# Attention edge layer: a third row and index buffer, and a block's steps taken in another order

## The chip, the cores and the metric

The kernel is one program on one core of a Trainium2 chip. The metric is device time in microseconds (us); lower is better. Engines are named as the profile names them: PE is TensorE (PEld its weight loads), DVE is VectorE, ACT is ScalarE, POOL is GpSimd, SP is SyncE.

## What is computed

Four graph layers run over the same 106,250 edges, sorted by destination, and 6,250 nodes. The change touches the edge part of the second, a graph attention layer with 8 heads:

```python
h = (x @ W.T).reshape(n, heads, out_dim)
a_s = jnp.sum(h * att_src, axis=-1)
a_d = jnp.sum(h * att_dst, axis=-1)
logits = jax.nn.leaky_relu(a_s[src] + a_d[dst], NEG_SLOPE)
m = jax.ops.segment_max(logits, dst, num_segments=n)
e = jnp.exp(logits - m[dst])
den = jax.ops.segment_sum(e, dst, num_segments=n)
alpha = e / (den[dst] + 1e-16)
out = jax.ops.segment_sum(alpha[:, :, None] * h[src], dst, num_segments=n)
```

## The kernel before, in words

`edges_gat` (L1017) takes the edges in 832 tiles of 128; 4 tiles are a group, 4 groups are a block, so there are 52 blocks. A node's edges stand together. All 16 tiles of a block are worked on together in its maxima; all else goes group by group.

For each block, POOL issues 16 indirect gathers (L1118), one a tile: 128 rows of 264 floats, the 256 features and the 8 source logits. Group b may be gathered into a buffer once `windows` has used the group b that lay there (L1112 to L1113). Then:

- **One-hots.** DVE's `select` (L1219) makes a 128x128 one-hot for each tile, edge against destination within the tile's window of 128 nodes. PE's `transpose` (L1393) turns it, ACT's `copy_sel` (L1133) copies the turned group out of PSUM, and PE's `expand` (L1401) multiplies it with the window's rows (loaded by SP, L1093) into destination logits in `att_ps`.
- **Maxima.** ACT copies the source logits (`copy_src`, L1162), PE's `values` (L1355) turns them, DVE's `tile_maxima` (L1231) scans them, PE's `tile_ends` (L1359) and DVE's `carries` (L1241) pass maxima from tile to tile, PE's `carry_lanes` (L1365) and DVE's `maxima` (L1254) finish them, PE's `edge_maxima` (L1371) turns them back. DVE's `logits_of` (L1271) forms logit minus maximum; ACT's `weights` (L1146) is the exp. PE's `falls` and `spread` and ACT's `shrink` make the factor by which a node that began in the block before is rescaled.
- **Sums.** DVE's `message` (L1289) multiplies a group's rows by the weights. PE's `windows` (L1413) multiplies rows and weights by the one-hots into `psa`, one PSUM bank a tile, 4 tiles. DVE's `add` (L1298) adds each of the four banks to the window in the accumulator `acc`; for group 0 it rescales one column first. `psa` has no second buffer: `windows` of a tile waits for the `add` of the same tile four tiles before.

Every engine runs its own hand-written order, tied to the others by semaphores. In a step, c is the coming block (one-hots), m the block in its maxima, a the one before m. `staggered` (L166) runs the steps in a hardware loop of two steps a turn, after two that stand outside it. The order on DVE before is: select c0; message a3; add a1; tile_maxima m; add a2; carries m; select c1; add a3; maxima m; select c2; logits_of m; select c3; message m0, m1, m2; add m0. PE follows it, with windows a2 and a3 at the head of its step and windows m0 and m1 at its end.

Of the kernel before, what the change touches and what calls it, by code (L numbers as in the profile page):

```python
# [28 lines left out]
PLANES = KH + 1  # L29
TILES = 832  # L30
# [135 lines left out]
def staggered(eng, step, lag, count=CHUNKS, peel=PEEL):  # L166


    def outside(s):
        step(lambda j: Chunk(s - j) if 0 <= s - j < count else None)  # L170

    for s in range(peel):
        outside(s)
    with eng.Fori(0, (count - peel) // 2) as pairs:
        for q in range(2):
            step(lambda j: Chunk(peel + q - j, pairs))
    for s in range(count, count + lag):
        outside(s)
# [838 lines left out]
def edges_gat(nc, dram, sh, acc):  # L1017
# [4 lines left out]
    with Phase(nc, "l1") as ph:  # L1022
# [3 lines left out]
        one = ph.sb("one", [HEADS, TILES])  # L1026
        pass_on, pass_back = ph.sb("pass_on", [HEADS, 2, TILES]), ph.sb("pass_back", [HEADS, TILES])
        rows = [ph.sb(f"rows{i}", [P, SEG, DW]) for i in range(2)]
        idx = [ph.sb(f"idx{i}", [P, SEG], I32) for i in range(2)]
        sel = [ph.sb(f"sel{i}", [P, SEG, P]) for i in range(2)]  # L1030
        wx = [ph.sb(f"wx{i}", [P, SEG, P]) for i in range(2)]
# [25 lines left out]
        gathered = [S(f"gathered{i}") for i in range(2 * NB)]  # L1057
# [7 lines left out]
        val_done = S("val_done", 1)  # L1065
# [9 lines left out]
        win_done = S("win_done", 2 * NB * GT)  # L1075
        added = S("added", GT)

        ph.begin()
        with nc.Block() as block:
# [24 lines left out]
            @block.gpsimd  # L1104
            def _(pool):
                def indices(n, q):
                    nc.gpsimd.tensor_copy(idx[q][:, :], sh["src_sb"][:, bass.ds(n * SEG, SEG)]).then_inc(idx_done, 1)

                def tiles(n, q, more):
                    hold(pool, ph, idx_done, n + 1)  # L1110
                    for b in range(NB):
                        hold(pool, ph, win_done, (n * NB + b + 1) * GT)  # L1112
                        if b == NB - 1 and more:  # L1113
                            hold(pool, ph, val_done, n + 1)
                            indices(n + 1, 1 - q)
                        for t in range(GT):
                            j = b * GT + t
                            nc.gpsimd.indirect_dma_start(  # L1118
                                out=rows[q][:, j, :], out_offset=None, in_=dram["tab1"][:, :],
                                in_offset=bass.IndirectOffsetOnAxis(ap=idx[q][:, j:j + 1].bitcast(U32), axis=0),  # L1120
                            ).then_inc(gathered[q * NB + b], 16)

                indices(0, 0)
                with pool.Fori(0, ITERS // 2 - 1) as pair:
                    for q in range(2):
                        tiles(pair * 2 + q, q, True)
                for q in range(2):
                    tiles(ITERS - 2 + q, q, q == 0)

            @block.scalar  # L1130
            def _(act):
# [14 lines left out]
                def weights(c):  # L1146
                    act.wait_ge(logits, c.n + 3)
                    nc.scalar.activation(wx[c.p][:, :, 0:HEADS], diff[c.p][:, :].rearrange("p (t h) -> p t h", h=HEADS),
                                         ACT.Exp).then_inc(w_done, 1)
# [12 lines left out]
                def copy_src(c):  # L1162
                    for b in range(NB):
                        act.wait_ge(gathered[c.p * NB + b], c.k * 64 + 64)
                    act.wait_ge(logits, c.n + 1)
                    nc.scalar.activation(src_v[c.p][:, :].rearrange("p (t h) -> p t h", h=HEADS), rows[c.p][:, :, D:DW],
                                         ACT.Copy).then_inc(src_done, 1)

                def step(at):
                    if at(1):  # L1170
                        copy_src(at(1))
                        copy_att(at(1))
                    if at(0):
                        copy_sel(at(0), 0)
                        copy_sel(at(0), 1)
                        copy_sel(at(0), 2)
                    if at(1):
                        weights(at(1))
                        shrink(at(1))
                    if at(0):  # L1180
                        copy_sel(at(0), 3)

                staggered(act, step, 1, ITERS, 2)

            @block.vector
            def _(dve):
# [14 lines left out]
                for w in wx:  # L1201
                    nc.vector.memset(w[:, :, :], 0.0)
# [17 lines left out]
                def select(c, b):  # L1220
                    g = c.n * NB + b
                    dve.wait_ge(win_done, (g + 1) * GT)
# [5 lines left out]
                def tile_maxima(c):  # L1228

                    dve.wait_ge(val_done, c.n + 2)  # L1230
# [40 lines left out]
                def logits_of(c):  # L1271
# [6 lines left out]
                    nc.vector.tensor_tensor(wx[c.p][:, :, HEADS:W2], by_tile(val_ps),  # L1278
# [10 lines left out]
                def message(c, b):  # L1289
# [4 lines left out]
                    m = rows[c.p][:, part, 0:D].rearrange("p t (h n) -> p t h n", n=HID)  # L1294
                    nc.vector.tensor_tensor(m, m, wx[c.p][:, part, 0:HEADS].unsqueeze(3).to_broadcast([P, GT, HEADS, HID]),
                                            ALU.mult).then_inc(msg_done, 1)

                def add(c, b, rescale=False):  # L1298
# [11 lines left out]
                    for t in range(GT):  # L1310
                        dve.wait_ge(win_done, (g + 2 * NB) * GT + t + 1)
# [5 lines left out]
                def step(at):  # L1317
                    c, m, a = at(0), at(1), at(2)
                    if c:
                        select(c, 0)  # L1320
                    if a:
                        message(a, 3)
                        add(a, 1)
                    if m:
                        tile_maxima(m)
                    if a:
                        add(a, 2)
                    if m:
                        carries(m)
                    if c:  # L1330
                        select(c, 1)
                    if a:
                        add(a, 3)
                    if m:
                        maxima(m)
                    if c:
                        select(c, 2)
                    if m:
                        logits_of(m)
                    if c:  # L1340
                        select(c, 3)
                    if m:
                        message(m, 0)
                        message(m, 1)
                        message(m, 2)
                        add(m, 0, True)

                staggered(dve, step, 2, ITERS, 2)

            @block.tensor  # L1350
            def _(pe):
# [7 lines left out]
                def tile_ends(c):  # L1359
                    pe.wait_ge(ends_done, c.n + 1)  # L1360
                    pe.wait_ge(carry_done, c.n + 1)
# [53 lines left out]
                def windows(c, b):  # L1415
                    g = c.n * NB + b
                    pe.wait_ge(msg_done, g + 1)
                    for t in range(GT):
                        j = b * GT + t
                        pe.wait_ge(added, g * GT + t + 1)  # L1420
                        for k in range(PLANES):
                            col = t * 512 + k * P
                            left = rows[c.p][:, j, k * P:(k + 1) * P] if k < KH else wx[c.p][:, j, :]
# [3 lines left out]
                def step(at):  # L1427
# [3 lines left out]
                    if a:  # L1431
                        windows(a, 2)
                    if c:
                        transpose(c, 0)
                    if a:
                        windows(a, 3)
                    if m:
                        tile_ends(m)
# [3 lines left out]
                    if m:  # L1442
                        carry_lanes(m)
                    if c:
                        expand(c, 1)
                    if m:
                        edge_maxima(m)
                    if c:
# [3 lines left out]
                    if c:  # L1452
                        expand(c, 2)
                        transpose(c, 3)
                    if m:
                        spread(m)
                        windows(m, 0)
                    if c:
                        expand(c, 3)
                    if m:  # L1460
                        windows(m, 1)

                staggered(pe, step, 2, ITERS, 2)


# [1089 lines left out]
```

## Time and profile before

| | |
|---|---|
| median of 3 runs | 7143.38 us (7141.86 to 7150.58) |
| profiled execution | 7181.66 us, span 7179.8 us, mean granted clock 0.764 |
| busy in the span | PE 66%, PEld 54%, DVE 58%, ACT 21%, POOL 49% |
| first gather to last `add` of the attention edge layer | 1906.8 to 3820.0 us |

In a row that groups instructions, the number after x is their count, the two after the bar are busy time in us and mean ns of one, and the last part is the idle time of the engine before them and what ended it. "remote" there means that the semaphore's update came more than 1.5 us after the recorded end of every instruction that could have made it; "issue" means that no semaphore is seen to have ended the wait. In a row of a timeline, the first number is the start, the second the time taken, in us, and the brackets hold the idle time before.

### The profile page before, as it was taken

Reading aid. Unit: us, or ns where it says so; the run is one execution under the profiler, and the core shown is the slowest. Engines: PE = TensorE matmul, PEld = TensorE weight load, DVE = VectorE, ACT = ScalarE, POOL = GpSimd, SP = SyncE. Lnnn points to the kernel's source line nnn. Section 1 sums busy time; section 2 is a strip of 40 time slices with the busy share of each in tenths; the row PEclk is TensorE's granted clock in tenths of the full one; section 3 lists DMA queues with packets and bytes.
Section 4 is the critical chain, followed back from the end, with each engine's and each line's share of the span. In section 5 each row is a group of like instructions: output and inputs, shape, how many; then the busy total and the mean of one; then the engine's idle time right before and its main releaser. Section 6 shows DMA issues by size and latency. Waiting matters only on the chain. (4 is left out here: it accounts for less than half of the span.)

```text
span 7179.8 us, 102208 instructions
## 1 busy us (share of the span) xinstructions
PE 4745.8 (66%) x25629; PEld 3906.0 (54%) x25629; DVE 4169.3 (58%) x11124; ACT 1511.2 (21%) x2515; POOL 3494.5 (49%) x3663
## 2 busy tenths in 40 slices
PE   4999999998577777777766566666664333333594
PEld 3777777776466666666665466666553222222232
DVE  3888888886555555555557555555554333333573
ACT  2666565663100000000003100000011000000370
POOL 1666666661344444444440466666634666666103
PEclk8999999999777777777777777777776555555695
DMA  4333333332222222222224323223232111111142
GB/s 156 90 91 91 91 92 91 90 90 86 86 70 65 69 67 71 65 69 68 69 67 122 93 85 86 85 85 86 85 86 67 22 22 23 22 22 22 48 116 77
DMA packets 417663, 536.60 MB, mean 75 GB/s; under 512 B 200355, under 2 KB 289701, under 8 KB 417477
## 3 DMA queue, kind: packets, MB, share of 16 engines
q0 software_dynamic: 154912, 381.74, 19.9%
q1 hardware_dynamic: 262566, 153.11, 8.1%
q14 instruction: 156, 1.28, 0.1%
q8 instruction: 29, 0.48, 0.0%
HBM read 482.55 MB, written 58.81 MB: 75 GB/s over the span
## 5 line engine op out<-in xcount | busy, mean ns | idle before, releaser
L457 POOL DMA_INDIRECT l_rows<-tmp_tab,l_idx x2496 | 2457.1, 984 | 1373.2 <-issue 710.0
L1873 PE MATMUL l_psa<-l_sel,l_rows 128*128 128x128 f32 (+1 forms) x4992 | 1092.6, 370 | 1319.8 <-DVE l_sel L475 1035.2
L1873 PEld LDWEIGHTS l_psa<-l_sel,l_rows 128*128 128x128 f32 (+1 forms) x4992 | 927.0, 244 | 1426.1 <-issue 794.3
L1118 POOL DMA_INDIRECT l_rows<-tmp_tab,l_idx x832 | 837.1, 1006 | 1004.2 <-PE l_psa L1424 758.1
L1840 DVE TENSOR_TENSOR acc<-acc,l_psa 128x256 f32 (+1 forms) x1664 | 584.0, 351 | 1206.6 <-issue 542.7
L757 PE MATMUL l_psw<-l_fw,l_ssp 128*128 128x256 f32 x3328 | 785.4, 389 | 50.7 <-DVE l_msg L657 48.9
L1424 PE MATMUL l_psa<-l_sel,l_rows 128*128 128x128 f32 x3328 | 631.3, 320 | 194.6 <-DVE acc L1315 145.5
L757 PEld LDWEIGHTS l_psw<-l_fw,l_ssp 128*128 128x128 f32 x3328 | 626.2, 193 | 220.3 <-DVE l_msg L657 77.6
L1315 DVE TENSOR_TENSOR acc<-acc,l_psa 128x384 f32 x832 | 461.4, 555 | 378.9 <-PE l_psa L1424 254.6
L1424 PEld LDWEIGHTS l_psa<-l_sel,l_rows 128*128 128x128 f32 x3328 | 525.7, 225 | 232.5 <-DVE acc L1315 173.4
L475 DVE TENSOR_SCALAR l_sel<-iota,rel 128x128 f32<-128x128 f32 x1664 | 386.5, 294 | 177.4 <-issue 135.3
L770 PE MATMUL l_psa<-l_sel,l_msg 128*128 128x128 f32 x3328 | 433.9, 278 | 69.0 <-DVE acc L677 67.5
L770 PEld LDWEIGHTS l_psa<-l_sel,l_msg 128*128 128x128 f32 x3328 | 410.9, 191 | 102.3 <-DVE acc L677 89.7
L1138 ACT ACTIVATE l_sel_t<-l_pst 128x512 f32<-128x512 f32 x208 | 124.2, 597 | 1405.8 <-DMA n_X<-in_x 877.6
L1411 PE MATMUL l_att_ps<-l_win,l_sel_t 128*128 128x8 f32 x1664 | 306.8, 312 | 168.4 <-ACT l_sel_t L1138 160.7
L1877 PE MATMUL l_psc<-l_sel,ones 128*128 128x128 f32 x1664 | 402.6, 330 | 7.1 <-issue 7.1
L657 DVE TENSOR_TENSOR l_msg<-l_psw,l_fb 128x512 f32<-128x512 f32 x416 | 285.8, 687 | 200.8 <-remote 100.6
L1411 PEld LDWEIGHTS l_att_ps<-l_win,l_sel_t 128*128 128x128 f32 x1664 | 294.2, 266 | 182.7 <-ACT l_sel_t L1138 167.7
L606 ACT ACTIVATE l_mag<-l_psz,l_fb 128x512 f32<-128x512 f32 x416 | 261.4, 679 | 591.5 <-PE l_psz L744 517.1
L677 DVE TENSOR_TENSOR acc<-acc,l_psa 128x256 f32 x832 | 346.3, 416 | 54.5 <-remote 38.7
L1424 PE MATMUL l_psa<-l_sel,l_wx 128*128 128x128 f32 x1664 | 364.5, 305 | 0.0
L1877 PEld LDWEIGHTS l_psc<-l_sel,ones 128*128 128x128 f32 x1664 | 330.9, 246 | 7.4 <-issue 7.2
(310 smaller groups left out, 6389.3 us busy)
## 6 DMA issues: line engine op xcount, KB each, us to landing
l_rows<-tmp_tab,l_idx POOLq DMA_INDIRECT x3328
l_edge<-in_edge_t SPq DMA_DIRECT2D x104, 256.0 KB
tmp_x<-n_X SPq DMA_DIRECT2D x39, 512.0 KB, 2.9
n_X<-in_x SPq DMA_DIRECT2D x26, 512.0 KB, 4.7
tmp_tab<-n_O POOLq DMA_DIRECT2D x26, 512.0 KB
l_win<-tmp_att_tab SPq DMA_DIRECT2D x832, 8.0 KB
n_X<-tmp_x SPq DMA_DIRECT2D x26, 512.0 KB, 3.5
l_lo_b<-tmp_lo_row SPq DMA_DIRECT2D x52, 256.0 KB
```

The costliest lines, as they stand in the source:

```text
L457: nc.gpsimd.indirect_dma_start(out=rows[b][:, t, :], out_offset=None, in_=table[:, :], in_offset=bass.IndirectOffsetOnAxis(ap=idx[q][:, j: ...
L475: last = nc.vector.tensor_scalar(sel[:, t, :], sh["iota"][:, :], col, None, ALU.is_equal)
L677: nc.vector.tensor_tensor(a, a, psa[:, t * D:(t + 1) * D].rearrange("p (k r) -> p k r", k=KH), ALU.add).then_inc(added, 1)
L757: last = nc.tensor.matmul(psw[:, t * D:(t + 1) * D], ssp[b % 2][:, k, t * P:(t + 1) * P], fw2[:, k, :], start=(k == 0), stop=(k == KH - 1))
L770: last = nc.tensor.matmul(psa[:, t * D + k * P:t * D + (k + 1) * P], msg[b % 2][:, t, k * P:(k + 1) * P], sel[b][:, t, :], start=True, sto ...
L1118: nc.gpsimd.indirect_dma_start(out=rows[q][:, j, :], out_offset=None, in_=dram["tab1"][:, :], in_offset=bass.IndirectOffsetOnAxis(ap=idx[q ...
L1315: nc.vector.tensor_tensor(a, a, part, ALU.add).then_inc(added, 1)
L1411: last = nc.tensor.matmul(att_ps[:, col:col + HEADS], sel_t[b % 2][:, t, :], win[b][:, t, HEADS:W2], start=True, stop=True)
L1424: last = nc.tensor.matmul(psa[:, col:col + P], left, sel[c.p][:, j, :], start=True, stop=True)
L1840: nc.vector.tensor_tensor(a, a, p, ALU.add).then_inc(added, 1)
L1873: last = nc.tensor.matmul(psa[0:n, col:col + P], rows[b][:, t, f:f + n], sel[b][:, t, :], start=True, stop=True)
L1877: last = nc.tensor.matmul(psc[:, col:col + P], sh["ones"][:, :], sel[b][:, t, :], start=True, stop=True)
```

## The change

The gathered rows and their indices have three buffers in place of two, so a gather of block n waits for the windows of block n-3. The space comes from `wx`, which is packed to 16 columns a tile (2,048 columns before, 368 now), and from `one`, which now lies in a one-hot buffer. The loops of POOL, ACT, DVE and PE take six steps a turn (`in_turns`), 8 turns in all, with four blocks' steps ahead of them; SP's is left as it was. The order of a step on DVE, ACT and PE is new. `tile_ends` gets a wait for the rescaling of the block before. Starting values of `val_done` and `win_done` follow the third buffer. No instruction of a step is added or removed.

```diff
+class Turn(Chunk):
+    def __init__(self, base, turns=None):
+        super().__init__(base, None if turns is None else turns * RING)
+        self.r = base % RING
+        self.kr = base // RING if turns is None else turns * 2 + base // RING
...
+    peel = count % TURN
+    for s in range(peel):
+        outside(s)
+    with eng.Fori(0, count // TURN) as turns:
+        for q in range(TURN):
+            step(lambda j: Turn(peel + q - j, turns))
...
-        rows = [ph.sb(f"rows{i}", [P, SEG, DW]) for i in range(2)]
-        idx = [ph.sb(f"idx{i}", [P, SEG], I32) for i in range(2)]
+        rows = [ph.sb(f"rows{i}", [P, SEG, DW]) for i in range(RING)]
+        idx = [ph.sb(f"idx{i}", [P, SEG], I32) for i in range(RING)]
...
-        wx = [ph.sb(f"wx{i}", [P, SEG, P]) for i in range(2)]
+        wx = [ph.sb(f"wx{i}", [P, SEG * W2 + P - W2]) for i in range(2)]
...
-        val_done = S("val_done", 1)
+        val_done = S("val_done", 2)
...
-        win_done = S("win_done", 2 * NB * GT)
+        win_done = S("win_done", RING * NB * GT)
... (ACT)
+                    c, m = at(0), at(1)
+                    if m:
+                        copy_src(m)
+                        copy_sel(m, 3)
+                        copy_att(m)
+                    if c:
+                        copy_sel(c, 0)
+                        copy_sel(c, 1)
+                        copy_sel(c, 2)
+                    if m:
+                        weights(m)
+                        shrink(m)
... (DVE)
                     c, m, a = at(0), at(1), at(2)
+                    if m:
+                        tile_maxima(m)
+                    if a:
+                        message(a, 2)
+                        add(a, 0, True)
                     if c:
                         select(c, 0)
+                    if m:
+                        carries(m)
                     if a:
                         message(a, 3)
                         add(a, 1)
+                    if c:
+                        select(c, 1)
                     if m:
-                        tile_maxima(m)
+                        maxima(m)
                     if a:
                         add(a, 2)
...
                     if c:
                         select(c, 2)
                     if m:
                         logits_of(m)
+                    if a:
+                        add(a, 3)
                     if c:
                         select(c, 3)
                     if m:
                         message(m, 0)
                         message(m, 1)
-                        message(m, 2)
-                        add(m, 0, True)
... (PE)
                     pe.wait_ge(ends_done, c.n + 1)
+                    if not (isinstance(c.n, int) and c.n == 0):
+                        pe.wait_ge(scaled, c.n)
...
                     if m:
                         values(m)
                     if a:
-                        windows(a, 2)
+                        windows(a, 0)
+                    if m:
+                        tile_ends(m)
+                        expand(m, 3)
+                    if a:
+                        windows(a, 1)
                     if c:
                         transpose(c, 0)
+                    if m:
+                        carry_lanes(m)
                     if a:
-                        windows(a, 3)
-                    if m:
-                        tile_ends(m)
+                        windows(a, 2)
                     if c:
                         expand(c, 0)
                         transpose(c, 1)
                     if m:
-                        carry_lanes(m)
+                        edge_maxima(m)
+                    if a:
+                        windows(a, 3)
                     if c:
                         expand(c, 1)
-                    if m:
-                        edge_maxima(m)
-                    if c:
                         transpose(c, 2)
                     if m:
                         falls(m)
                     if c:
                         expand(c, 2)
-                        transpose(c, 3)
                     if m:
                         spread(m)
-                        windows(m, 0)
                     if c:
-                        expand(c, 3)
-                    if m:
-                        windows(m, 1)
+                        transpose(c, 3)
```

## Rows read from the trace of the kernel before

**Rows 1.** Stretches: PE, PEld, DVE, ACT, POOL busy us (instructions), PE clock, DMA share, GB/s.

```profile
2500.00:3000.00 500.00, 355.99 (x2210) 321.68 (x2208) 293.96 (x756) 47.58 (x126) 221.63 (x238) 0.74 0.28 69
```

**Rows 2.** All instructions of `values` (L1357), one a block.

```profile
L1357 PE MATMUL l_val_ps<-ident,l_src_v x52: 272/273/454, 1970.2 to 3788.5; 128*128 128x128 f32 x52
```

**Rows 3.** Groups of instructions of some 44 blocks, 2112.0 to 3673.8 us.

```profile
L1118 POOL DMA_INDIRECT l_rows<-tmp_tab,l_idx x694 | 680.0, 980 | 852.3 <-PE l_psa L1424 648.2 <-issue 189.3 <-remote 10.1
L1315 DVE TENSOR_TENSOR acc<-acc,l_psa 128x384 f32 x693 | 384.3, 555 | 315.9 <-PE l_psa L1424 212.7 <-issue 33.9 <-remote 25.3
L1276 DVE TENSOR_TENSOR l_logit<-l_src_v,l_att 128x128 f32<-128x128 f32 x44 | 12.8, 290 | 70.6 <-remote 62.9 <-PE l_val_ps L1373 6.5 <-issue 1.2
L1258 DVE TENSOR_TENSOR l_lanes<-l_tile_of,l_psm 128x32 f32<-128x32 f32 x44 | 8.1, 184 | 73.5 <-remote 71.9 <-issue 1.5
L1246 DVE COPY l_chain<-l_chain 8x1 f32<-8x1 f32 x43 | 6.1, 142 | 78.9 <-PE l_psm L1362 52.4 <-DMA tmp_att_tab<-n_A 26.5
L1224 DVE TENSOR_SCALAR l_sel<-iota,rel 128x128 f32<-128x128 f32 x698 | 156.5, 296 | 83.3 <-issue 71.6 <-PE l_psa L1424 11.1
```

**Rows 4.** Timeline of DVE within one block.

```profile
2819.20 0.41 DVE L1233 TENSOR_TENSOR_SCAN l_scan<-l_pen,l_val_ps 128x128 f32<-128x128 f32 x1
2819.96 0.19 DVE L1238 TENSOR_TENSOR l_ends<-l_tile_of,l_scan 128x32 f32<-128x32 f32 x1
...
2827.15 0.14 DVE L1246 COPY l_chain<-l_chain 8x1 f32<-8x1 f32 x1 [1.18 <-PE l_psm L1362]
...
2827.61 0.15 DVE L1250 TENSOR_TENSOR_SCAN l_chain<-l_pass_back,l_psm 8x15 f32<-8x15 f32 x1
...
2829.12 2.62 DVE L1315 TENSOR_TENSOR acc<-acc,l_psa 128x384 f32 x4 [0.42 <-issue]
2831.65 0.18 DVE L1258 TENSOR_TENSOR l_lanes<-l_tile_of,l_psm 128x32 f32<-128x32 f32 x1
...
2833.18 0.87 DVE L1224 TENSOR_SCALAR l_sel<-iota,rel 128x128 f32<-128x128 f32 x4
2837.56 0.29 DVE L1276 TENSOR_TENSOR l_logit<-l_src_v,l_att 128x128 f32<-128x128 f32 x1 [3.51 <-remote]
...
2838.62 0.29 DVE L1286 TENSOR_TENSOR l_diff<-l_lrelu 128x128 f32<-128x128 f32 x1
...
2839.63 3.49 DVE L1295 TENSOR_TENSOR l_rows<-l_rows,l_wx 128x1024 f32<-128x1024 f32 x3
...
2843.10 0.14 DVE L1308 TENSOR_TENSOR acc<-acc,l_alpha 8x1 f32 x1
```

**Rows 5.** Timeline of PE: first two at 1.2, then two at 2.4 GHz; last two 1.2.

```profile
2807.81 1.22 PE L1424 MATMUL l_psa<-l_sel,l_rows 128*128 128x128 f32 x4
...
2809.26 1.06 PE L1424 MATMUL l_psa<-l_sel,l_rows 128*128 128x128 f32 x4
...
2813.99 0.61 PE L1424 MATMUL l_psa<-l_sel,l_rows 128*128 128x128 f32 x4
...
2814.66 0.61 PE L1424 MATMUL l_psa<-l_sel,l_rows 128*128 128x128 f32 x4
...
2830.64 1.88 PE L1411 MATMUL l_att_ps<-l_win,l_sel_t 128*128 128x8 f32 x8 [0.20 <-ACT l_sel_t L1138]
2834.11 1.11 PE L1399 MATMUL l_pst<-ident,l_sel 128*128 128x128 f32 x4 [0.31 <-issue]
```

**Rows 6.** Timeline of all engines in the next block, around the end of its gathers.

```profile
2865.06 0.40 PE L1368 MATMUL l_psm<-l_chain,l_head_t 8*128 8x32 f32 x2
...
2869.26 0.95 POOL L1118 DMA_INDIRECT l_rows<-tmp_tab,l_idx  x1 [0.30 <-issue]
2871.87 0.19 DVE L1258 TENSOR_TENSOR l_lanes<-l_tile_of,l_psm 128x32 f32<-128x32 f32 x1 [4.47 <-remote]
```

**Rows 7.** Timeline of DVE and POOL as the layer begins.

```profile
1963.48 0.95 POOL L1118 DMA_INDIRECT l_rows<-tmp_tab,l_idx  x1 [0.30 <-issue]
...
1970.67 0.42 DVE L1233 TENSOR_TENSOR_SCAN l_scan<-l_pen,l_val_ps 128x128 f32<-128x128 f32 x1 [26.77 <-PE l_val_ps L1357]
```

## What the change will do: the prediction

> **What bounds the kernel now.** I looked first at the page's busy shares. No engine is full over the span, so a stage has to be read by itself. The stretches inside the attention edge layer show PE busy for 356 of 500 us, DVE for 294, POOL for 222, with the clock at 0.74 of full [rows 1]. So there too nothing is full: the layer waits on handovers. Its period comes from `values`, which runs once a block: (3788.5 - 1970.2) / 51 = 35.65 us [rows 2].
>
> Next, the groups of the layer show who waits. Per block (44 blocks, 43.3 by the count of adds) DVE idles 7.3 us before `add`, 1.6 before the logits, 1.7 before `maxima`, 1.8 before `carries` and 1.9 before `select` [rows 3]. POOL idles 852 us and four fifths of that is waiting for `windows`; still, nothing is seen to wait for the gathers, and POOL with 16 x (0.98 + 0.30) = 20.5 us a block is no bound. So the third buffer alone would buy nothing.
>
> Third, DVE's timeline gives what a step takes when nothing holds it [rows 4]: a `select` 0.87, x4 = 3.5; a `message` 3.49 / 3 = 1.16, x4 = 4.65; an `add` of four tiles 0.42 to load its addresses and 2.62, x4 = 12.2; the rescale 0.1 (the last `message` ends at 2843.12, the rescale at 2843.24); `tile_maxima` 2819.20 to 2820.15, 0.95; `carries` 2827.15 to 2827.76, 0.6; `maxima` 2831.65 to 2833.18, 1.5; `logits_of` 2837.56 to 2838.91, 1.35. Sum 24.9 us. The other 35.65 - 24.9 = 10.75 us a block is waiting, and it agrees with the groups: 7.3 - 3.3 (the gaps inside the four adds, already in the 12.2) + 1.6 + 1.7 + 1.8 + 1.9 = 11.0.
>
> **Part by part.**
>
> *The order of the step.* Before, DVE asks PE for something and has little to do until it comes: after `tile_maxima` only add a2, which itself waits for PE; after `maxima` only one `select`. In the new order each of the three handovers has cover on DVE: between `tile_maxima` and `carries` a message, an add and a select, 1.16 + 3.04 + 0.87 = 5.1 us; between `carries` and `maxima` the same, 5.1; between `maxima` and the logits an add and a select, 3.9. The plain wait before `carries` (1.8 us) goes. Laid end to end, DVE is done with `tile_maxima` at 0.95 us of the step, message a2 at 2.1, add a0 5.3, select c0 6.1, carries 6.8, message a3 7.9, add a1 11.0, select c1 11.8, maxima 13.4, add a2 16.4, select c2 17.3, logits 18.6, add a3 21.7, select c3 22.5, messages m0 and m1 24.9. Against it stands PE at 2.4 GHz, with the durations of the next paragraph. Windows a0 starts when message m0 ends, 1.2 us before the step, and is ready at 1.5 (wanted from 2.5). `tile_ends` and expand m3 follow the rescale, to 3.5, and windows a1, which needs the banks that add a0 has emptied, is ready at 6.0 (wanted from 8.3). Transpose c0 and `carry_lanes` end at 7.4; windows a2 follows add a1 bank by bank, to 11.7 (from 13.8); expand c0, transpose c1 and `edge_maxima` end at 13.9 (17.3); windows a3 follows add a2 to 17.1 (19.0). PE is ahead everywhere, so at full clock the step is DVE's 24.9 us.
>
> *PE's clock.* A tile of `windows` takes 2814.66 - 2813.99 = 0.67 us at 2.4 GHz and (2809.26 - 2807.81), less the 0.2 us by which the first row starts early, about 1.28 at 1.2 GHz; an `expand` takes 1.88 and a `transpose` 1.11 at 1.2 GHz [rows 5] and near half of that at 2.4. A step of PE is 16 x 0.67 + 4 x 1.0 + 4 x 0.6 + 2.7 for the small ones = 20 us at full clock, 16 x 1.28 + 4 x 1.88 + 4 x 1.11 + 3.1 = 35.5 us at half. Now the clock is at 0.74, near half of the time at each level. With 20 us of work in under 30 and no wait as long as the present ones, it should stay up for more of the time, but not always: with the half-speed durations in the same walk `edge_maxima` ends at 19.8, 2.5 us late, and the last bank of windows a2 is 0.4 late. I take 1.0 us a block (0 to 10.6, PE's 35.5 less 24.9).
>
> *PE's signals while gathers run.* `carry_lanes` ended by the record at 2865.46, with DVE idle for it, and DVE went on only at 2871.87. POOL's eighth gather in a row had been issued by 2870.21 [rows 6]. The waits called remote, 71.9 of 73.5 us before `maxima` and 62.9 of 70.6 before the logits [rows 3], are of this kind: 3.2 us a block. It looks as if PE's updates are held until a run of gathers has drained, some 1.6 us after the last issue. In the new order `windows` frees four gathers at a time, a fourth of a step apart. Four take 4 x 1.28 = 5.1 us, so the runs get shorter and a held signal waits less, against 3.9 to 5.1 us of cover. I take 1.1 us left of these (0 to 6.4 for each handover), and 2.0 of the 4.0 before `add`, for they are partly held signals too.
>
> *The wait in `tile_ends`.* It now waits for the rescale, which DVE does 1.2 us after `tile_maxima`; queued behind it on PE are expand m3 and windows a1, needed 5 us later. Nothing, at most 1 us a block.
>
> *The loops.* The first `select` of a turn on DVE waits for no semaphore: 71.6 us of "issue" over 22 turns [rows 3], 3.3 us for each jump back, 1.65 a block. With six blocks a turn it is 0.55. The Trainium skill ("Runtime: NRT & Kernel Launch", Instruction fetch mechanics) says that a taken branch whose target is outside the buffered window makes the engine fetch before it can go on. It gives PE a buffer of 2,048 instructions. The trace agrees on DVE. By that page PE would begin to stall too, for its loop goes from some 640 matmuls and loads (4,418 in 500 us) to 1,900, and more with its waits; it would be 3.3 x 8 = 26 us if nothing covered it, and as DVE and PE jump at about the same time I add nothing for it.
>
> *The third buffer at the start.* POOL issues 32 gathers without a pause until 1964.43, and DVE gets its first value from PE at 1970.67 after 26.8 idle us [rows 7]. Now three blocks are free, so 48 gathers run on: 16 x 1.28 = 20 us later. I add 20 once (0 to 20).
>
> *Small things.* `wx` is cleared by two memsets of 368 columns for 2,048: 3 us less. SP's loads for the next block follow `expand` and have most of a step of slack: nothing, below 1 us either way.
>
> **The sum.** A block: 24.9 + 0.55 + 1.0 + 1.1 + 2.0 = 29.6 us, against 35.65: 6.05 less, x 51 = 309. Less 20 at the start, plus 3: 292 us. From the profiled execution's 7181.7 that is 6890. The median shown is 38 us lower, so 7143 - 292 = 6851, say **6850 us**.
>
> **The rivals.**
>
> *A part of it only.* Held signals and a slow clock keep 7 us of waits, a block of 32.5: 3.15 x 51 - 17 = 144, so 7000 us. For it: no step of PE is shorter, and POOL needs 20.5 us plus a drain of 1.6 after each run of four, 27 us a block, so gathers are in flight nearly always. Against: each handover has its 4 to 5 us.
>
> *Slower, by signals held all through.* Now POOL pauses for a third of each block, and in that pause PE's signals are prompt. With a third buffer the gathers spread over the step. If four gathers follow four without a drain between them, PE's eight handovers of a step (values, ends, lanes, maxima and four windows) are all late. If the waits reach 12 us a block, the period is 37.5: +1.85 x 51 + 17 = 111, so 7255 us. It decides from 9.9 us of waits a block, 1.2 us beyond cover at each of the eight. Against it: the next four gathers wait for `windows`, which come through PE's own held signal, so POOL has to pause and drain.
>
> *PE at 1.2 GHz all along.* Then PE is the bound with 35.5 us a block: no gain and the start lost, 7155 us. Against it: now the clock rises within a block, to 2.4 GHz between the windows at 2809.26 and those at 2813.99 [rows 5], and after the change PE has the same run of work in less time.
>
> *The change does what it says, but to no end*: the third buffer takes waiting from POOL, which nothing waits for. That holds for the buffer; the reordering has its own effect, so this falls together with the case above.
>
> *Better.* Only 1 us of waits left, 26.4 a block: 9.2 x 51 - 17 = 452, 6690 us.
>
> **How the numbers follow.** The forecast (27.6 to 31.3 a block, 6750 to 6940 us) 0.55; better than that 0.08; a part only (to 7128) 0.20; near nothing, with PE at the slow clock, 0.05; slower 0.12. The range 6720 to 7120 leaves out the slower case, the case of nothing and a tail of the better one. 0.2% is 14 us, about what a measurement of this kernel can tell from no change: faster 0.83, same 0.05, slower 0.12.
>
> **What would show it.** After the change `values` should come every 29 to 30 us. DVE should idle no longer before `carries`, and under 1 us a block before `maxima` and the logits; the waits called remote should shrink. The idle time before `select` should fall from 71.6 us to a third. PE's clock should be above 0.74 in the layer. DVE's first wait should grow to some 45 us. The forecast is wrong if remote waits before `add` grow by more than what the others lose, if the clock falls, or if POOL's gathers run on without pauses.

## The result: 4.2% faster, and the profile after

The changed kernel takes 6840.3 us, median of four runs (6834.6 to 6859.2), against 7142.6 us for the kernel before (four runs, 7139.2 to 7150.6). The ratio is 0.958, with a 95% interval of 0.956 to 0.960. The forecast was 6850.

The profiled execution took 6859.2 us with a span of 6857.4; before, the span was 7179.8. That is 322.4 us less, and the two traces split it into three parts. From the first gather to the end of the last `add`, the layer took 1913.2 us before and 1618.6 after: 294.6 us less. The work ahead of it, which the change doesn't touch, is 7.2 us shorter (first gather at 1906.8 and at 1899.6), and the work behind it 20.6 us. So the layer accounts for nearly all of it.

The page's busy times show nearly the same work (PE is busy 2% less, DVE 0.4% less than before) in a shorter span:

```profile
PE 4632.1 (68%) x25629; PEld 3837.0 (56%) x25629; DVE 4151.1 (61%) x11124; ACT 1512.4 (22%) x2515; POOL 3542.8 (52%) x3663
```

The same stretch as in [rows 1], in the trace after:

```profile
2500.00:3000.00 500.00, 400.44 (x2654) 370.19 (x2653) 345.04 (x905) 55.97 (x147) 284.15 (x285) 0.80 0.34 83
```

PE has 2654 matmuls in 500 us where it had 2210, and DVE 905 instructions for 756: both 1.20 times as many. The granted clock rose from 0.74 to 0.80. Next come `values` on PE, where [rows 2] stood, and the first instruction of `logits_of` on DVE, one each per block (count, shortest, median and longest ns, first and last start). The last row is that of the logits before:

```profile
L1387 PE MATMUL l_val_ps<-ident,l_src_v x52: 417/421/477, 1942.3 to 3481.6; 128*128 128x128 f32 x52
L1305 DVE TENSOR_TENSOR l_logit<-l_src_v,l_att x52: 273/285/298, 1990.0 to 3496.9; 128x128 f32<-128x128 f32 x52
```

```profile
L1276 DVE TENSOR_TENSOR l_logit<-l_src_v,l_att x52: 281/292/294, 1977.9 to 3801.0; 128x128 f32<-128x128 f32 x52
```

PE now makes the first block's values at 1942.3, long before DVE uses them, so `values` would give 30.2 us. I take the period from DVE's logits: (3496.9 - 1990.0) / 51 = 29.55 us a block. The row before gives (3801.0 - 1977.9) / 51 = 35.75, against the 35.65 of [rows 2].

The groups from 2112 to 3500 us, some 47 blocks, answer to [rows 3] (busy us, mean ns, then the idle time just before them and what ended it):

```profile
L1147 POOL DMA_INDIRECT l_rows<-tmp_tab,l_idx x723 | 757.9, 1048 | 502.4 <-PE l_psa L1456 295.5 <-issue 201.5 <-remote 4.7
L1344 DVE TENSOR_TENSOR acc<-acc,l_psa 128x384 f32 x750 | 415.3, 554 | 256.7 <-remote 69.4 <-issue 65.9 <-PE l_psa L1456 51.0
L1324 DVE TENSOR_TENSOR l_rows<-l_rows,l_wx 128x1024 f32<-128x1024 f32 x188 | 223.9, 1212 | 34.3 <-ACT l_wx L1177 25.9 <-issue 8.3
L1253 DVE TENSOR_SCALAR l_sel<-iota,rel 128x128 f32<-128x128 f32 x736 | 167.9, 304 | 0.0
L1262 DVE TENSOR_TENSOR_SCAN l_scan<-l_pen,l_val_ps 128x128 f32<-128x128 f32 x47 | 19.7, 419 | 57.5 <-PE l_val_ps L1387 49.1 <-issue 4.4 <-remote 3.8
L1305 DVE TENSOR_TENSOR l_logit<-l_src_v,l_att 128x128 f32<-128x128 f32 x47 | 13.4, 286 | 54.7 <-remote 53.5 <-issue 1.1
L1287 DVE TENSOR_TENSOR l_lanes<-l_tile_of,l_psm 128x32 f32<-128x32 f32 x47 | 8.5, 180 | 0.8 <-remote 0.8
L1275 DVE COPY l_chain<-l_chain 8x1 f32<-8x1 f32 x47 | 6.7, 142 | 0.0
```

Three waits of [rows 3] are gone: before `select` (83.3), `carries` (78.9) and `maxima` (73.5). Before the logits 54.7 us remain, 1.2 a block. Before `add` there are 256.7 / 46.9 = 5.5 us a block, for 7.3. Two small waits are new: 1.2 us a block before `tile_maxima` (L1262), and 0.7 before `message` (L1324), which waits for ACT's weights. Before, they came to 2.5 and 3.2 us in the whole stretch. POOL's wait for `windows` fell from 648.2 to 295.5 us.

The start of the layer, in DVE's timeline, where [rows 7] stood:

```profile
1961.76 0.42 DVE L1262 TENSOR_TENSOR_SCAN l_scan<-l_pen,l_val_ps 128x128 f32<-128x128 f32 x1 [29.35 <-issue]
...
1968.05 0.14 DVE L1275 COPY l_chain<-l_chain 8x1 f32<-8x1 f32 x1 [4.52 <-issue]
...
1986.35 0.19 DVE L1287 TENSOR_TENSOR l_lanes<-l_tile_of,l_psm 128x32 f32<-128x32 f32 x1 [17.04 <-remote]
...
1990.03 0.29 DVE L1305 TENSOR_TENSOR l_logit<-l_src_v,l_att 128x128 f32<-128x128 f32 x1 [1.27 <-PE l_val_ps L1405]
```

And POOL's last gather of the opening run:

```profile
1979.27 0.95 POOL L1147 DMA_INDIRECT l_rows<-tmp_tab,l_idx  x1 [0.30 <-issue]
```

`maxima` of the first block starts only at 1986.35, 6.1 us after the last of 48 gathers had been issued. The first logits come 90.4 us after the first gather; before it was 71.1. So the start costs 19.3 us. But the delay isn't in DVE's first wait, which is 29.4 us (26.8 before): `tile_maxima` starts at 1961.76 and `carries` at 1968.05, in the middle of POOL's run. It stands before `maxima`, 17.0 us.

### The profile page after: what moved, and what is told of

Read it like the earlier page. It is cut to its first block and busy times, and to the rows that moved or that the text cites. A ratio compares the mean times of both kernels' runs of the same rounds, so it can differ in the third digit from the quotient of the medians.

```text
span 6857.4 us, 101777 instructions
## 1 busy us (share of the span) xinstructions
PE 4632.1 (68%) x25629; PEld 3837.0 (56%) x25629; DVE 4151.1 (61%) x11124; ACT 1512.4 (22%) x2515; POOL 3542.8 (52%) x3663
## 3 DMA queue, kind: packets, MB, share of 16 engines
q0 software_dynamic: 154912, 381.74, 20.5%
## 5 line engine op out<-in xcount | busy, mean ns | idle before, releaser
L484 POOL DMA_INDIRECT l_rows<-tmp_tab,l_idx x2496 | 2453.9, 983 | 1377.4 <-issue 695.6
L1147 POOL DMA_INDIRECT l_rows<-tmp_tab,l_idx x832 | 886.3, 1065 | 577.5 <-PE l_psa L1456 339.4
L1443 PE MATMUL l_att_ps<-l_win,l_sel_t 128*128 128x8 f32 x1664 | 270.9, 290 | 162.4 <-ACT l_sel_t L1167 152.0
L1443 PEld LDWEIGHTS l_att_ps<-l_win,l_sel_t 128*128 128x128 f32 x1664 | 261.9, 240 | 174.7 <-ACT l_sel_t L1167 161.4
```

The source lines that it names most:

```text
L484: nc.gpsimd.indirect_dma_start(out=rows[b][:, t, :], out_offset=None, in_=table[:, :], in_offset=bass.IndirectOffsetOnAxis(ap=idx[q][:, j: ...
L1147: nc.gpsimd.indirect_dma_start(out=rows[r][:, j, :], out_offset=None, in_=dram["tab1"][:, :], in_offset=bass.IndirectOffsetOnAxis(ap=idx[r ...
L1443: last = nc.tensor.matmul(att_ps[:, col:col + HEADS], sel_t[b % 2][:, t, :], win[b][:, t, HEADS:W2], start=True, stop=True)
```

## The experiments

All twelve ran after the first pair, in three sets on two chips, and there the kernel before takes 6300 to 6306 us, not 7143. No wait in any of their traces is called remote, so whatever makes PE's signals late in the first pair is absent. (I call such signals held.) Each kernel is compared with the kernel before of its own set. The period is that of the logits; the layer runs from the first gather to the last `add`.

| kernel | median us (kernel before) | ratio, 95% interval | period us | layer us |
|---|---|---|---|---|
| before_again | 6305.8 (6306.3), one run | | 30.55 | 1632.5 |
| loops_only | 6220.0 (6300.1) | 0.987, 0.9855 to 0.9888 | 28.85 | 1543.0 |
| old_order | 6221.0 (6300.1) | 0.987, 0.9853 to 0.9886 | 28.99 | 1550.0 |
| ring2 | 6262.5 (6300.1) | 0.994, 0.9919 to 0.9952 | 29.73 | 1588.7 |
| short_start | 6015.9 (6300.1) | 0.955, 0.9531 to 0.9563 | 24.82 | 1338.7 |
| after_again | 6019.8 (6306.3) | 0.955, 0.9533 to 0.9565 | 24.95 | 1345.5 |
| early_values | 6022.0 (6306.3) | 0.955, 0.9531 to 0.9562 | 25.00 | 1348.5 |
| half_gathers | 6017.8 (6306.3), one run | | 24.79 | 1342.6 |
| after_third | 6020.2 (6302.5) | 0.955, 0.9535 to 0.9561 | 24.94 | 1345.2 |
| half_again | 6019.5 (6302.5), one run | | 24.82 | 1345.0 |
| hot1 | 5970.3 (6302.5) | 0.947, 0.9457 to 0.9483 | 24.10 | 1301.4 |
| hot2 | 5918.0 (6302.5) | 0.939, 0.9373 to 0.9398 | 22.99 | 1245.5 |

### The kernels before and after where no signal is held

before_again and after_again are the two kernels unchanged.

> The kernel before, for a trace beside those of the other experiments, in which no wait was ended by a late signal of PE. If the held signals cost what the first traces say, its period is near 24.9 + 1.65 + 1.8 + 2 = 30.4 us here against 35.75, with no idle time called remote. Rival, that the traces only differ in how they tell of it: 35 us again.

> The changed kernel. Without held signals the order alone acts: 24.9 us a block and a short wait before tile_maxima, 25.2 us, so 5 us a block less than before and 270 us in all. With held signals again: 29.5 us and 302 us less. Rival, that the gain was the held signals': less than half of 302 where there are none.

The periods are 30.55 and 24.95 us, and the gain is 286.5 us. The groups of before_again, 1800 to 3100 us, 42 blocks:

```profile
L1315 DVE TENSOR_TENSOR acc<-acc,l_psa 128x384 f32 x680 | 377.1, 555 | 220.9 <-PE l_psa L1424 134.2 <-issue 32.1 <-DVE acc L1315 4.2
L1224 DVE TENSOR_SCALAR l_sel<-iota,rel 128x128 f32<-128x128 f32 x676 | 153.0, 293 | 78.4 <-PE l_psa L1424 66.4 <-issue 11.4
L1276 DVE TENSOR_TENSOR l_logit<-l_src_v,l_att 128x128 f32<-128x128 f32 x42 | 11.9, 283 | 0.0
L1258 DVE TENSOR_TENSOR l_lanes<-l_tile_of,l_psm 128x32 f32<-128x32 f32 x42 | 7.6, 180 | 0.0
L1246 DVE COPY l_chain<-l_chain 8x1 f32<-8x1 f32 x43 | 6.1, 142 | 78.7 <-PE l_psm L1362 78.7
```

And of after_again, same stretch, 51 blocks:

```profile
L1344 DVE TENSOR_TENSOR acc<-acc,l_psa 128x384 f32 x825 | 456.8, 554 | 184.9 <-DVE acc L1344 64.1 <-issue 60.2 <-PE l_psa L1456 14.7
L1262 DVE TENSOR_TENSOR_SCAN l_scan<-l_pen,l_val_ps 128x128 f32<-128x128 f32 x50 | 20.5, 410 | 21.7 <-PE l_val_ps L1387 21.7
L1305 DVE TENSOR_TENSOR l_logit<-l_src_v,l_att 128x128 f32<-128x128 f32 x51 | 14.5, 284 | 0.0
L1275 DVE COPY l_chain<-l_chain 8x1 f32<-8x1 f32 x50 | 6.9, 137 | 0.0
```

In the old order the waits before `maxima` and the logits are already zero when no signal is held. What the change removes here, loops included, is 1.9 us a block before `select`, 1.8 before `carries` and 1.6 before `add`. So the gain doesn't need held signals: it is nearly as large without them, though not made of the same waits. The step falls to 24.95 us, near the 24.9 that the prediction laid end to end from [rows 4]. The stretch 2500 to 3000 us, in before_again and then in after_again:

```profile
2500.00:3000.00 500.00, 412.42 (x2598) 380.91 (x2597) 344.20 (x880) 54.67 (x146) 266.00 (x278) 0.73 0.32 80
```

```profile
2500.00:3000.00 500.00, 431.01 (x3163) 401.88 (x3163) 410.68 (x1081) 67.85 (x180) 340.12 (x341) 0.86 0.40 99
```

DVE is busy 411 of 500 us, before 344, and the granted clock is 0.86 where it was 0.73. A block of 24.95 us has 24.95 x 410.68 / 500 = 20.5 us of DVE's work and the 3.3 us of gaps inside the adds, which leaves 1.2 us for everything else. That makes DVE the likely bound; hot1 and hot2 below test it.

### The three parts of the change, apart

loops_only keeps the order and the two buffers and takes the six-step turns, with the packed `wx`, whose clearing is 3 us shorter. Against the kernel before:

```
+RING = 2
+TURN = 6
...
-                staggered(dve, step, 2, ITERS, 2)
+                in_turns(dve, step, 2, ITERS)
...
```

> Two buffers and the order of before, with only the loops of six steps a turn, the packed wx and one in sel. My theory, that DVE stood 3.3 us at each jump back with nothing beside it: 24 jumps become 8, 16 x 3.3 = 53 us less, 7090 us. Rival, that the jump stood beside waits that stay: 7140 us.

old_order is the changed kernel, three buffers and six-step turns, with the order of before on ACT, DVE and PE. Against the changed kernel, like all edits from here on:

```
+                    if c:
+                        select(c, 0)
+                    if a:
+                        message(a, 3)
+                        add(a, 1)
...
-                        message(a, 2)
-                        add(a, 0, True)
...
+                        message(m, 2)
+                        add(m, 0, True)
...
-                    if not (isinstance(c.n, int) and c.n == 0):
-                        pe.wait_ge(scaled, c.n)
```

> The changed kernel with three buffers and six-step loops, but the order of before on ACT, DVE and PE, without the new wait in tile_ends. My theory, that nothing waits for the gathers: no gain over loops_only and 20 us lost at the start, 7110 us. Rival, that the third buffer carries the gain by spreading the gathers: under 6950 us.

ring2 is the changed kernel with two buffers:

```
-RING = 3
-TURN = 2 * RING
+RING = 2
+TURN = 6
...
-        val_done = S("val_done", 2)
+        val_done = S("val_done", 1)
...
-                    dve.wait_ge(val_done, c.n + 3)
+                    dve.wait_ge(val_done, c.n + 2)
```

> The new order with six-step loops, but two buffers. My theory, that the order carries the gain: the last gathers of a block are then released by windows a3, 17 us into the step, take 5 and drain in 1.6, and copy_src wants them at 25: a little late in some blocks, 31 us a block for 29.6, 6900 us. Rival A, that the order needs the buffer: over 7050 us. Rival B, that the buffer buys nothing at all: 6820 us, the shorter start.

The loops alone give 80 us, more than I expected. There are 25 - 8 = 17 jumps fewer, so 4.7 us each. In loops_only's groups (1800 to 3100 us, 45 blocks) the wait before `select` fell from 1.9 to 0.4 us a block, and the one before `carries` from 1.8 to 1.3. Both rows name PE. But the wait before `select` comes once a turn in both kernels: in before_again every second block, 3.6 us, in loops_only every sixth, 2.7 to 2.9. And `carries` in before_again waits 2.5 us in one block of each turn and 1.2 in the other. So a jump cost 3.6 + 1.3 = 4.9 us there, which fits the 4.7:

```profile
L1344 DVE TENSOR_TENSOR acc<-acc,l_psa 128x384 f32 x718 | 398.1, 554 | 251.6 <-PE l_psa L1453 163.2 <-DVE acc L1344 38.9 <-issue 20.0
L1253 DVE TENSOR_SCALAR l_sel<-iota,rel 128x128 f32<-128x128 f32 x720 | 162.1, 302 | 20.1 <-PE l_psa L1453 19.5
L1275 DVE COPY l_chain<-l_chain 8x1 f32<-8x1 f32 x45 | 6.4, 142 | 58.3 <-PE l_psm L1391 58.3
```

The third buffer in the old order gives nothing: 6221 against 6220. The new order without the third buffer is 42 us worse than the old one, so the rival that the order needs the buffer is right. Both together give 201 us (6221 to 6020; 205 to short_start, which ran in the same set). The row that explains it, ring2 in the same stretch, 43 blocks:

```profile
L1262 DVE TENSOR_TENSOR_SCAN l_scan<-l_pen,l_val_ps 128x128 f32<-128x128 f32 x43 | 18.1, 421 | 217.7 <-PE l_val_ps L1387 217.7
```

DVE waits 5.0 us a block before `tile_maxima`. `values` needs all 16 gathers of its block through `copy_src`, and with two buffers they start only as the block before last frees its groups, which the new order does in the middle and at the end of the step. The third buffer moves them a block ahead. Among the instructions of `l_src_v` in ring2, what ended ACT's idle time (us, times):

```profile
  DMA l_rows<-tmp_tab,l_idx: 463.9, 52
```

ACT waits for gathered rows in every block. In after_again the same row has 13.2 us in three.

### The start, and values a step earlier

short_start keeps the third buffer from being filled until the first block's values are out:

```
-        val_done = S("val_done", 2)
+        val_done = S("val_done", 1)
...
-                    dve.wait_ge(val_done, c.n + 3)
+                    dve.wait_ge(val_done, c.n + 2)
```

> The changed kernel, but the index copy of a block waits for values of the block two before it, not three (val_done starts at 1), so at the start POOL stops after two blocks of gathers. My theory, that PE's signals are held as long as gathers run on: the first logits come 20 us earlier and nothing else changes, 6820 us. Rival, that the start is bound by something else, or that the loss comes back as waits of POOL in each block: 6840 us or more.

It takes 6015.9 us, ratio 0.9547 to after_again's 0.9549: the same. But the changed kernel has no late start here: after_again has 51.0 us from the first gather to the first logits, before_again 55.7. So the 19.3 us of the first pair were seen only where signals are held. short_start had nothing to remove and doesn't test them.

early_values puts `copy_src` at the end of ACT's step and `values` ahead of the last transposes on PE:

```
                 def step(at):
...
-                        copy_src(m)
...
+                    if c:
+                        copy_src(c)
...
-                    if m:
-                        values(m)
...
+                        values(c)
```

> The changed kernel, with copy_src of the coming block at the end of ACT's step and its values on PE ahead of the last transpose. If the 1.2 us of DVE's wait before tile_maxima is PE's order, it goes: 40 to 60 us below the changed kernel where signals are held, 15 where they are not (0.4 us a block in that trace). Rival, that it is the rescaling and the signals: no difference.

The wait before `tile_maxima` went, from 21.7 to 3.6 us in 50 blocks, and the kernel isn't faster:

```profile
L1345 DVE TENSOR_TENSOR acc<-acc,l_psa 128x384 f32 x832 | 460.8, 554 | 206.2 <-DVE acc L1345 61.9 <-issue 61.4 <-PE l_psa L1457 39.5
L1263 DVE TENSOR_TENSOR_SCAN l_scan<-l_pen,l_val_ps 128x128 f32<-128x128 f32 x50 | 20.5, 410 | 3.6 <-issue 3.6
```

But the adds wait 39.5 us for PE where they waited 14.7 in after_again: the wait has only moved. The timelines tell what it is. In after_again the 21.7 us are seven waits of 2.3 to 3.4 us, one in each turn of six blocks. Each time PE had nothing to wait for and yet was late with the first instruction of its turn, `values`:

```profile
2136.77 0.47 PE L1387 MATMUL l_val_ps<-ident,l_src_v 128*128 128x128 f32 x1 [3.66 <-issue]
...
2137.47 0.42 DVE L1262 TENSOR_TENSOR_SCAN l_scan<-l_pen,l_val_ps 128x128 f32<-128x128 f32 x1 [3.27 <-PE l_val_ps L1387]
```

In early_values `values` runs ahead of the jump, and PE has the same gap before the new first instruction of its turn, `windows` a0:

```profile
2146.26 1.22 PE L1457 MATMUL l_psa<-l_sel,l_rows 128*128 128x128 f32 x4 [3.72 <-issue]
```

So it is PE's own jump back. Before `values`, PE idles 2.5 to 3.8 us once a turn in after_again and 1.6 to 2.5 in loops_only, but in before_again, with two steps in the loop, never above 0.5 us in 48 blocks. The longer loop on PE brought this stall. What is left before `tile_maxima` in early_values is 0.5 us a turn.

### Half the gathers

half_gathers and half_again are the same kernel on the two chips: it issues every second gather and leaves the other tiles' rows at zero.

```
-                        for t in range(GT):
+                        for t in range(0, GT, 2):
```

> The changed kernel with every second gather left out: only even tiles are gathered, rows of odd tiles are zeros from one memset, and the semaphores count accordingly. If gathers in a run are what holds PE's signals, the period falls to 25 us where after_again has 29.5, and stays at 25 where it has 25. Rival, that DVE's waits come from PE's clock: no change in either case. The three memsets cost some 10 us at the start.

> The changed kernel with every second gather left out (rows of odd tiles are zeros). Tells something only where PE's signals are held: a period of 25 us if gathers in a run hold them, 29.5 us if not. Elsewhere 24.9 us again.

The semaphore that ACT waits for counts half as many, and three memsets clear the rows. They take 6018 and 6020 us, the same as the changed kernel. POOL's groups in half_gathers, 1800 to 3100 us:

```profile
L1147 POOL DMA_INDIRECT l_rows<-tmp_tab,l_idx x388 | 376.1, 969 | 665.7 <-PE l_psa L1458 582.5 <-issue 83.1
```

Half the work of POOL and little over half the traffic (55 GB/s from 2500 to 3000 us, for 99) buy nothing, so neither is a bound where signals aren't held. It was meant to show whether shorter runs of gathers free PE's signals. With none held, it can't: that question is open.

### Taking work from DVE

If DVE is the bound, moving one-hots to ACT must pay. hot1 moves `select` of group 3, hot2 of groups 1 and 3 (both with short_start's edit). ACT makes each tile's |rel - iota| and then Relu(1 - that):

```
+                    for t in range(GT):
+                        last = nc.scalar.activation(dif[:, t, :], sh["iota"][:, :], ACT.Abs, scale=-1.0,
+                                                    bias=sh["rel"][:, bass.ds(g * GT + t, 1)])
...
+                    nc.scalar.activation(sel[c.p][:, b * GT:(b + 1) * GT, :], dif[:, :, :], ACT.Relu,
+                                         scale=-1.0, bias=1.0).then_inc(hot_done, 1)
```

> The changed kernel, to stand beside the other three. 0.955 of before where no signals are held, 0.958 where they are.

> short_start with group 3 alone made by ACT. DVE as the bound: 0.87 us a block, 45 us below the changed kernel. If PE takes over, hot2 gives no more than this one.

> short_start with the one-hots of groups 1 and 3 made by ACT (Abs of iota minus the edge's place, four times, then Relu of one minus that over the group), so DVE does two selects a step for four. If DVE's 24.9 us are the bound, 2 x 0.87 us a block go, 90 us below the changed kernel where no signals are held. Rival, that PE is the bound already (20 us at the full clock, more with its slow stretches): 30 us or less. Rival, that ACT, with some 4 us more a block, comes late with its copies: no gain.

They take 5970.3 and 5918.0 us against 6020.2: 50 and 102 us less, a little more than the 0.87 us per group and block that `select` takes (45 and 90). The columns below are PE, PEld, DVE, ACT and POOL. In hot2, DVE issues 975 instructions for the 1081 of after_again, and ACT is busy 141 us instead of 68:

```profile
2500.00:3000.00 500.00, 433.31 (x3262) 407.21 (x3262) 405.39 (x975) 141.24 (x380) 309.63 (x310) 0.87 0.40 99
```

```profile
L1271 DVE TENSOR_SCALAR l_sel<-iota,rel 128x128 f32<-128x128 f32 x396 | 93.2, 318 | 0.0
L1362 DVE TENSOR_TENSOR acc<-acc,l_psa 128x384 f32 x828 | 458.4, 554 | 169.0 <-issue 54.6 <-DVE acc L1362 26.2 <-PE l_psa L1473 16.6
```

hot2's layer ends at 2972.7, so the last 27 us of that stretch belong to what follows. From 2500 to 2950 DVE is busy 372 us in hot2 and 369 in after_third: it stays as full as before. The adds' waits don't grow, so the step simply shortens with DVE's work, and DVE is the bound. hot2 beats both kernels, 0.939 of the kernel before. It wasn't run where signals are held.

## Why the prediction was right

Step by step, against the forecast's terms:

- **The period**: 29.6 us forecast, 29.55 measured. The layer: 292 us less forecast, 294.6 measured.
- **The order of the step.** Right. The waits before `carries` and `maxima` are gone. With no signal held the step is 24.95 us, against the dense 24.9; part of that agreement is chance, for the measured work and gaps are 20.5 + 3.3 = 23.8, and 1.2 us are waits. Laid end to end, single durations count the overlap of neighbours twice: in [rows 4] the adds of 2829.12 take 2.62 us, to 2831.74, and `maxima` starts at 2831.65. What the step missed is that this holds only with the third buffer. I wrote "So the third buffer alone would buy nothing", which old_order confirms. But I gave the buffer no part in the order's gain either, and ring2 shows that without it the order loses 42 us. In the walk I wanted `windows a0` by 2.5 us and never asked when the gathers for `values` would be in. The number came out right because the change has both.
- **Waits not foreseen.** 1.2 us before `tile_maxima` and 0.7 before `message`. The walk let `tile_maxima` start at once. With no signal held 0.4 of the 1.2 remain, and they are PE's jump, as after_again and early_values show. The rest, and the whole wait before `message` (0.0 in after_again), occur only where signals are held; no run tells more of them.
- **The logits and the adds.** 1.1 us forecast for held signals, 1.2 measured before the logits, just above the "under 1 us" that the prediction named as a sign. For the adds I left 2.0 us beside the 3.3 of their gaps; measured 5.5 - 3.3 = 2.2.
- **The loops.** The size was off, and a term put at nothing was not nothing. I gave 1.1 us a block, 56 us in all; loops_only gives 80. I priced only the `select` behind the jump, by its 3.3 us; the wait before `carries` also falls, by 0.5 us a block. The `select` wait itself went to zero in the first pair, not to a third, for `select` no longer stands first in the step. For PE's longer loop I added nothing. The Trainium skill ("Runtime: NRT & Kernel Launch", Instruction fetch mechanics) gave reason to fear a stall of PE there, and the traces agree: PE idles up to 3.8 us at each jump with six steps in the loop and none with two. It costs DVE 21.7 us in seven turns of after_again, near the 26 that the prediction named and left out. That the 0.55 charged to DVE's jump isn't there, and this is, is luck.
- **PE's clock.** The direction was right, 0.74 to 0.80, and 0.73 to 0.86 where nothing is held. Its own cost, 1.0 us a block, isn't told apart from the other waits by any run; where nothing is held there is little room for it, with 1.2 us left in all and 0.4 of them PE's jump.
- **The start.** 20 us forecast, 19.3 measured in the first pair, and none elsewhere. The size was right and the place wrong: DVE's first wait was to grow to some 45 us and is 29.4. Signals of PE arrived at 1961.76 and 1968.05 with the run of 48 gathers still on until 1980.22; only the third, before `maxima`, came after it. So they aren't simply held until a run ends, and the agreement in size is partly luck.
- **Held signals.** With late signals the same kernel has a period of 35.75 us, without them 30.55, 5.2 us a block apart; after the change it is 29.55 and 24.95, 4.6 apart. That the late signals cost this is what the waits say: those before the logits and `maxima` are gone, and those before `add` fell from 7.3 to 5.2 us. That runs of gathers hold them is not shown, but the timelines say more than [rows 6]. In the kernel before, 35 of the 36 waits called remote before the logits and `maxima` (2112 to 3674 us) end 1.6 to 1.8 us after the last gather of a run of eight. After the change about half of the runs are of four, but some are longer: nine waits make up 44 of the 54.7 us before the logits, and eight of them follow runs of 11 or 12. Against it stand the start above, and the later sets: there POOL's runs are mostly of 8 to 16 gathers, and no signal is late. So a run of gathers is not enough by itself. Every run of an experiment came where none was held, so the rest couldn't be tried. The rival by which held signals would get worse is refuted for this change: they cost no more than before.
- **PE at 1.2 GHz, a part only.** Refuted: the period is 29.55 and the clock rose.

The sum is right partly because errors cancel. Measured, a block of 29.55 us is 29.55 x 345.04 / 500 = 20.4 of DVE's work, 3.3 of gaps, 2.2 before the adds, 1.2 before the logits, 1.9 of unforeseen waits and 0.5 of small ones. Against the forecast's 24.9 + 0.55 + 1.0 + 1.1 + 2.0, the dense sum was 1.2 too high, and the 1.55 for DVE's jump and the clock appeared nowhere as such. The unforeseen waits, with PE's jump in them, and the small ones took their place.

## What to carry to other kernels

When each engine waits in turn for the others, lay the bound engine's instructions end to end from one block's timeline: that sum (24.9 us here) is where a reordering can get, and the walk must also ask when every input arrives, the loads too. A buffer that nothing waits for (0 us alone) can be what a new order stands on (-42 us without it, 201 us with it), so test such parts alone and together. A longer hardware loop has fewer jumps, but each may cost more: look at the first instruction of a turn on every engine (on PE none with two steps, up to 3.8 us with six). Taking other work ahead of the jump only moves such a wait (early_values). When the bound engine is busy all through, moving its work to an idle engine pays in full (hot2, 102 us).

## What the hardware showed unexpectedly

The same kernel took 7142.6 us in the first pair and 6300 to 6306 us in all three later sets, on two chips: 12% less. All three stretches shorten: up to the first gather from 1906.8 to 1728.9 us, the layer from 1913.2 to 1632.5, the rest from 3359.8 to 2942.7. In the layer the difference goes with late signals: 62.9 and 71.9 us of waits called remote before the logits and `maxima` in [rows 3], none in before_again, and 2.1 us a block less before `add`. The instructions themselves take as long (a gather 0.946 us, an add 0.555 in both), and the granted clock over the layer is no higher in the faster run, 0.72 against 0.73. So in the layer it isn't the clock; why PE's signals come late in one place and not in the others, no run settled. The gain of the change is near the same in both, 302 and 286 us.
